# Attention over 64 heads in a fused four-layer kernel: probabilities kept in PSUM, cut to 16-bit halves there and turned by one DMA a head in place of TensorE

## The reference, cut to what matters

```python
# B = 2, T = 512, hidden 512, 32 heads, 8 KV heads (G = 4 heads each), head size 128, causal, RoPE
q = rope(x @ Wq.T); k = rope(x @ Wk.T); v = x @ Wv.T
scores = einsum('bkgtd,bksd->bkgts', q, k) / sqrt(128)
attn = softmax(where(causal, scores, -inf))
out = einsum('bkgts,bksd->bkgtd', attn, v)
return out @ Wo.T
```

## Time and profile before

| | |
|---|---|
| median of the runs | 2485.62 us (2484.69 to 2487.72) |
| profiled execution, its own time | 2484.75 us |
| its span, first to last instruction | 2482.8 us |
| busy over the span | PE 96%, PEld 55%, DVE 72%, ACT 64%, POOL 50% |
| attention stage, from the first turn to the last ohi | 1624.1 to 2325.9 us |
| granted TensorE clock, mean | 0.986 |

### The profile page before, as it was taken

How to read it: one execution, slowest core, us unless ns; L and a number is a source line. 1 busy time by engine, 2 the same in 40 slices (tenths; PEclk the granted TensorE clock), 3 DMA queues, 4 the chain that set the end, 5 groups by cost and what they waited for, 6 DMA issues and landing times. The chain is left out here.

```text
span 2482.8 us, 48888 instructions
## 1 busy us (share of the span) xinstructions
PE 2378.8 (96%) x15424; PEld 1368.9 (55%) x15624; DVE 1787.9 (72%) x3234; ACT 1591.7 (64%) x3327; POOL 1232.0 (50%) x986
## 2 busy tenths in 40 slices
PE   6999999999999999999999998879999999999797
PEld 3555555555555555555555555445555555555443
DVE  6777777777777777777777776577777777788522
ACT  7676776776776776776776775265665656656422
POOL 4455555555555556556556459344434343454223
PEclk8999999999999999999999999999999999999999
DMA  7343343343343343343343341230110110100000
GB/s 248 108 129 111 108 128 111 108 133 105 113 132 107 110 133 109 106 137 109 102 140 109 119 151 56 103 124 1 43 43 1 44 44 1 43 18 1 1 0 34
DMA packets 113827, 218.79 MB, mean 88 GB/s; under 512 B 9632, under 2 KB 43040, under 8 KB 111360
## 3 DMA queue, kind: packets, MB, share of 16 engines
q1 hardware_dynamic: 113536, 215.28, 26.6%
HBM read 212.10 MB, written 3.15 MB: 87 GB/s over the span
## 5 line engine op out<-in xcount | busy, mean ns | idle before, releaser
L256 DVE SCALAR_TENSOR_TENSOR xc<-bank,taps,xc 128x511 f32<-128x511 f32 (+2 forms) x384 | 284.7, 742 | 44.6 <-ACT xc L243 27.4
L984 ACT ACTIVATE E<-wq,cst 128x128 f32<-128x128 f32 x1024 | 311.8, 390 | 2.2 <-PEq L298 2.2
L1268 POOL TENSOR_TENSOR xw<-xt,wdec 128x384 f32<-128x384 f32 x128 | 106.4, 832 | 327.3 <-DVE xt L1119 163.7
L1277 POOL TENSOR_TENSOR acc<-acc,sq 128x512 f32<-128x512 f32 x112 | 172.0, 1536 | 186.8 <-ACT sq L996 186.8
L1911 POOL TENSOR_TENSOR qT<-qT,qrot 128x512 f32<-128x512 f32 x64 | 81.3, 1270 | 368.6 <-DVE qrot L1801 368.6
L1161 DVE SCALAR_TENSOR_TENSOR u<-xc,D,bank 128x512 f32<-128x512 f32 x128 | 95.6, 747 | 210.3 <-PE bank L813 198.8
L1100 DVE TENSOR_TENSOR E<-E,cbm 128x1024 f32<-128x1024 f32 x128 | 242.9, 1898 | 0.8
L61 PE MATMUL bank<-xhi,wx 128*128 128x512 f16 x640 | 242.5, 379 | 0.0
L60 PE MATMUL bank<-xlo,wx 128*128 128x512 f16 x640 | 242.5, 379 | 0.0
L59 PE MATMUL bank<-xhi,wx 128*128 128x512 f16 x640 | 242.5, 379 | 0.0
L1263 POOL TENSOR_TENSOR ecs<-ecs,xcC 128x768 f32<-128x768 f32 x128 | 234.1, 1829 | 0.4 <-POOLq L298 0.4
(11 more groups left out here) (237 smaller groups left out, 6299.4 us busy)
## 6 DMA issues: line engine op xcount, KB each, us to landing
wq<-cs_rows SPq DMA_DIRECT2D x128, 512.0 KB, 4.1
ecs<-ecs_rows SPq DMA_DIRECT2D x128, 384.0 KB, 3.6
wx<-in_w_xbc SPq DMA_DIRECT2D x80, 256.0 KB, 2.7
wz<-in_w_z SPq DMA_DIRECT2D x64, 256.0 KB, 2.7
wo<-in_w_o SPq DMA_DIRECT2D x64, 256.0 KB, 4.0
wq<-in_wq SPq DMA_DIRECT2D x8, 1024.0 KB, 5.7
awo<-in_wo SPq DMA_DIRECT2D x8, 1024.0 KB, 5.0
wkv<-in_wkv SPq DMA_DIRECT2D x8, 512.0 KB, 3.7
```

Source lines behind the costliest of these rows:

```text
L256: self.nc.vector.scalar_tensor_tensor(out=dst[:, d:T], in0=self.k.bank[bank][:, 0:T - d], scalar=self.taps[:, bass.ds(g, 1), b, j, 3 - d:4 ...
L984: ins = nc.scalar.activation(E[t.i % 4][:, h, c], sc.csr[t.i % 2][:, h, c * P:(c + 1) * P], ACT.Relu, scale=-1.0, bias=head(sc.cst, t, c, h))
L1277: nc.gpsimd.tensor_tensor(acc[t.b][:], acc[t.b][:], sq[:], ALU.add).then_inc(acc_done, 1)
```

## The change

1. Exponentials are written over the scores in PSUM (`scores_at`), and there are two homes for scores, one for even and one for odd heads (`S_AT`), in banks 2 to 6. The float32 probs in SBUF and `normalise` are gone.
2. ScalarE makes the leading halves straight from PSUM with the reciprocal as scale (`leading_p`), four instructions; VectorE makes the remainders, `rest_of_p`, four `scalar_tensor_tensor`: row block 1 at once, since the next scores share its bank, and the others after `maxima`.
3. Both halves go into one tile ph of 20 blocks of 128 columns, and one `dma_start_transpose` a head, issued by SP (`turn`), turns it into pt. TensorE's `turn`, pthi and ptlo are gone. `attend` reads pt; the remainders of one key block are five blocks apart.
4. New orders. TensorE: projection of Q, scores of n + 2, projections of K and V, output projection, attend. ScalarE: leading halves of p of n + 1, of q of n + 3, exps of n + 2, (k and v), and then ohi of n. VectorE: scales of n + 1, remainder of row block 1, rotation of q, maxima of n + 2, remaining remainders of n + 1, (k and v), addition of the output, and olo of n last.
5. The leading half of v comes straight from PSUM on ScalarE, its remainder from PSUM on VectorE in place of a copy; GpSimd's `rest_of_v` is gone.
6. SP's loads of SwiGLU weights are cut up, one or so an item in the first two groups, between transposes; the scale of the down projection is loaded in the SwiGLU stage, and VectorE multiplies it there later.

```diff
-P_OFF = [896, 1024, 512, 0]
-S_AT = [(3, 384), (4, 0), (3, 0), (2, 0)]
-T_OFF = [0, 512, 896, 1152]
-T_AT = [(5, 0), (6, 0), (5, 0), (5, 256)]
+P_BLOCKS = 20
+S_AT = [[(3, 384), (4, 0), (3, 0), (2, 0)], [(6, 384), (4, 256), (6, 0), (5, 0)]]
+HALVED = (1, 3, 2, 0)
...
-        pthi, ptlo = sb("pthi", [P, 1280], F16), sb("ptlo", [P, 1280], F16)
+        ph = [sb(f"phalves{i}", [P, P_BLOCKS * P], F16) for i in range(2)]
+        pt = [sb(f"pturned{i}", [P, P_BLOCKS, P], F16) for i in range(2)]
...
+        def leading_blocks(h, i):
+            return ph[h % 2][:].rearrange("p (b t) -> p b t", t=P)[:, i + 1:6 * i + 2:5, :]
+        def scores_at(h, i):
+            bank, at = S_AT[h % 2][i]
+            return k.bank[bank][:, at:at + (i + 1) * P]
+        def probs(h, i):
+            return scores_at(h, i).rearrange("p (b t) -> p b t", t=P)
...
+                def turn(n, h):
+                    sp.wait_ge(p_lo, n + 1)
+                    sp.sem_inc(step, 1)
+                    if not (isinstance(n, int) and n < 2):
+                        sp.wait_ge(pv_ready, n - 1)
+                        sp.sem_inc(step, 1)
+                    sp.dma_start_transpose(out=pt[h % 2][:], in_=ph[h % 2][:]).then_inc(pt_in[h % 2], 16)
...
                 def body(g, s, p):
+                    for b in range(NB):
+                        for h in range(QH):
+                            n = item(g, b, h)
+                            if later(g, b, h, 1):
+                                turn(n + 1, h + 1)
+                            if isinstance(g, int) and g < 2:
+                                load_swiglu(k, io, sp, n)
...
-                def scores(n, g, b, h, first=False):
+                def scores(n, g, b, h):
                     pe.wait_ge(q_lo, n + 1)
...
-                    if not first:
-                        pe.wait_ge(exp_done, n)
+                    wait(pe, p_lo, n - 1)
                     for i in (3, 2, 0, 1):
+                        if i == 1:
+                            wait(pe, p_lo1, n)
...
-                def attend(n, g, b):
+                def attend(n, g, b, h):
                     pe.wait_ge(pv_free, n + 1)
+                    pe.wait_ge(v_lo, (g * NB + b) + 1)
+                    pe.wait_ge(pt_in[h % 2], 16 * turned(g, b, h) + 16)
                     for j in range(CH):
...
+                        out = k.bank[7][:, j * P:T].rearrange("p (i t) -> p i t", t=P)
+                        mm = product(nc, out, (vhi[b][:, j], vlo[b][:, j]),
+                                     (pt[h % 2][:, 6 * j + 1:5 * j + 5], pt[h % 2][:, 6 * j:16 + j:5]), j == 0, j == CH - 1)
...
                             n = item(g, b, h)
-                            turn(n, h, [0], None)
-                            turn(n, h, [1], None)
-                            uses = ring_uses(g, b, h)
-                            for i, (kind, what) in enumerate(uses):
+                            for i, (kind, what) in enumerate(ring_uses(g, b, h)):
                                 ahead, bank = ring(g, b, h, i)
+                                ring_free(pe, ahead)
                                 if kind == "o":
...
                                     output(1 - b, bank, s if b else 1 - s, what)
+                                else:
...
+                                if kind == "q":
+                                    m = later(g, b, h, 2)
+                                    scores(item(*m), *m)
...
+                            attend(n, g, b, h)
...
-                def normalise(n, h):
+                def leading_p(n, h, of_parity):
                     act.wait_ge(exp_done, n + 1)
                     act.wait_ge(rsum_done, n + 1)
...
+                    wait(act, pt_in[h % 2], 16 * of_parity)
+                    for i in HALVED:
+                        nc.scalar.activation(leading_blocks(h, i), probs(h, i), ACT.Copy,
+                                             scale=rsum[h % 2][:, i:i + 1]).then_inc(p_hi, 1)
...
-                            for u, (bank, at, size) in enumerate(EVAC):
-                                if u == 2 and later(g, b, h, 1):
-                                    normalise(n + 1, h + 1)
-                                act.wait_ge(pt_ready, 3 * n + u + 1)
-                                nc.scalar.copy(pthi[:, at:at + size], k.bank[bank][:, 0:size]).then_inc(pt_hi, 1)
+                            if later(g, b, h, 1):
+                                leading_p(n + 1, h + 1, turned(g, b, h + 1))
                             if later(g, b, h, 3):
                                 leading_q(n + 3, h + 3)
+                            if later(g, b, h, 2):
+                                exps(n + 2, h + 2)
                             if h == 1 and not is_last(g, b):
                                 leading_k(g * NB + b + 1, 1 - b)
-                                leading_v(g * NB + b + 1, 1 - b)
+                                leading_v(g * NB + b + 1, 1 - b, *ring(g, b, h, 2))
                             act.wait_ge(pv_ready, n + 1)
                             nc.scalar.activation(ohi[b][:, h], k.bank[7][:, :], ACT.Copy,
                                                  scale=1.0 / P_SCALE).then_inc(ohi_done, 1)
-                            if later(g, b, h, 2):
-                                exps(n + 2, h + 2)
...
+                def rest_of_p(n, h, first):
+                    for i in HALVED[:1] if first else HALVED[1:]:
+                        dve.wait_ge(p_hi, 4 * n + (4, 1, 4, 2)[i])
+                        out = ph[h % 2][:, 5 * i * P:(6 * i + 1) * P].rearrange("p (b t) -> p b t", t=P)
+                        ins = nc.vector.scalar_tensor_tensor(out=out, in0=probs(h, i), scalar=rsum[h % 2][:, i:i + 1],
+                                                             in1=leading_blocks(h, i), op0=ALU.mult, op1=ALU.subtract)
+                    ins.then_inc(p_lo1 if first else p_lo, 1)
...
                                 scales(n + 1, h + 1)
-                            for u in range(2):
-                                rest_of_p(n, u)
+                                rest_of_p(n + 1, h + 1, True)
...
                                     serve(kind, ahead, bank, n + 3, 0, what[1], what[2])
...
                                 maxima(n + 2, h + 2)
+                            if later(g, b, h, 1):
+                                rest_of_p(n + 1, h + 1, False)
+                            for i, (kind, what) in enumerate(uses):
+                                ahead, bank = ring(g, b, h, i)
+                                if kind in "kv":
+                                    serve(kind, ahead, bank, 0, g * NB + b + 1, what[1], 0)
+                                elif kind == "o":
+                                    add_output(1 - b, ahead, bank, what, g * NB + b - 1)
                             dve.wait_ge(ohi_done, n + 1)
```

More of the change, by code:

```diff
@@ L1572, in ring, with ring_free @@
                 ahead -= QH
-            return (g * NB + b) * 10 + (PRO + ahead), (PRO + ahead) % 2
+            return (g * NB + b) * 10 + (PRO + ahead), k.bank[(PRO + ahead) % 2]
+        def ring_free(pe, ahead):
+            wait(pe, proj_free, ahead - 1)
         LAST_OUT = (NG * NB - 1) * 10 + (PRO - QH) + 5
@@ L1691, in body @@
-                            turn(n, h, [2, 3], 3 * n + 1)
-                            m = later(g, b, h, 2)
-                            if m:
-                                scores(item(*m), *m)
-                            attend(n, g, b)
-                            for i, (kind, what) in enumerate(uses):
-                                if kind == "o":
-                                    ahead, bank = ring(g, b, h, i)
-                                    pe.wait_ge(proj_free, ahead - 1)
@@ L1887, in body @@
                                                            op1=ALU.subtract).then_inc(pv_free, 1)
-                            for i, (kind, what) in enumerate(uses):
-                                if kind == "o":
-                                    ahead, bank = ring(g, b, h, i)
-                                    add_output(1 - b, ahead, bank, what, g * NB + b - 1)
                             if is_last(g, b):
@@ L2226, in program @@
                 attention(k, io, aw)
-            swiglu(k, out)
+            swiglu(k, io, out)
 def layouts(i):
```

194 lines of the change are left out of this document (83 added, 111 removed).

## The result

The changed kernel takes 2531.97 us (median of 4 runs, 2531.91 to 2532.07) against 2485.34 before (median of 4, one more than in the table above), a ratio of 1.0186 with a 95% interval of 1.0168 to 1.0204. It is slower by 46.6 us, where 2475 us, faster, was forecast; the range of 2440 to 2550 holds it. Spans differ by 2530.1 - 2482.8 = 47.3 us. The last ohi shows that all of it arises in the attention stage: it starts 49.2 us later than in the earlier trace rows.

A forecast was written before the change was run, and what follows sets the result against it. TensorE, busy 9.69 of 9.75 us, was taken as the bound, then a 9.5 us loop through the other engines. The attention stage's -10.3 us took 2484.75 to 2474.4; with 0.87 for the median, 2475 us, range 2440 to 2550.

The forecast's parts named there:

- What goes on TensorE: Ten turns (1.10 us) and a stall (0.1 us) leave each head: ordinary head 8.57 us on TensorE, some 77 us in all.
- the rival in which it keeps the pace: TensorE still bounds the attention stage: gain up to 77 us, 2408 us, or in part 2440; chance 0.12.
- The new loop: Chain through ScalarE, VectorE and GpSimd, exps through ohi to nmx, closes once a head: 9.5 us an ordinary head, against 9.75.
- The head with K and V: Output projection waits for the bank of k, then takes 2.72 us: head 15.55 us, against 14.96 before.
- The DMA transpose: 640 KB a head on SP's queue lands in 6 us (bounds 3.0 and 13.6), hidden up to 8.4 us.
- a late landing: Transpose lands later than 8.4 us and delays attend: 2507 us at a 10 us landing, 2568 at 13.6; chance 0.22.
- a bound queue: Transposes on SP's queue become the bound, 12.3 us a head, 787 us in place of 707: 2565 us; chance 0.06.
- Both ends: Attention stage from start to end: nmx(7) at 1685.5, last ohi at 2315.6 instead of 2325.9, that is -10.3 us.
- the interval before the last head: From nmx(62) to nmx(63), with moments (0.9 us) and no rotation (2.34 us): from 2292.7 to 2300.7.
- the loop longer than read: ScalarE and VectorE in the same banks as TensorE cost 0.3 us a head or more: 2490 to 2510 us; chance 0.13.

The follow-up runs named there:

- experiment 7: Changed kernel with attend right behind the scores, ohi ahead of exps, olo ahead of the output's addition: 2493.65 us; further variants added ring-order, GpSimd and last-unit changes.
- Experiment 2: Changed kernel with GpSimd's weight split ahead of the addition of q, and its remainder of q waiting until nmx is done: 2512.40 us.
- experiment 3: Changed kernel with the projection of V computed twice, filling TensorE's wait for the bank of k: 2513.71 us.
- experiment 4: Changed kernel with the ring in the order q, output, k, v instead of q, k, v, output: 2500.45 us.
- experiment 6: Changed kernel with each head's DMA transpose made twice, one after the other, attend waiting for the second: 2590.72 us.

## Why the prediction was wrong, by its own steps

- **What goes on TensorE** was right: 88% busy, not the bound. The rival in which it keeps the pace (2408 to 2440) did not come.
- **The new loop** was right as a mechanism (experiment 7), wrong in size: 10.1 us against 9.5. By terms, from the rows of after: exps to ohi 2.03 (2.02 forecast), so the exponentials in PSUM cost what those into SBUF did; ohi 0.63, olo 0.61, sums and reciprocal 0.38, to ScalarE and back 0.17 and 0.50 (0.09 and 0.45), row block 1 0.40, rotation 2.27 (2.34), and mask to nmx 2.58 + 0.51 where the sum had 2.61 with nmx in it. The term that failed is the last: nmx was priced from one row, which starts (1854.59) just as GpSimd's split ends there (1854.65), so the row doesn't show what nmx costs a little earlier in the split. That it can be longer was there to be read before the change: 20 of the 64 took 0.4 to 1.65 us. Experiment 2 gives 0.33 us of the 0.6 back (10.11 to 9.78). The rest is small latencies: 0.13 between the mask and the reductions, 0.08 and 0.05 above.
- **The head with K and V** was right in its structure, the output projection behind the bank of k, and in size in three heads of fourteen (15.8 against 15.55). In the other eleven it failed where that projection was priced at 2.72 us: behind 2.7 us of idle time the clock was at its lower level and it took 3.9 to 4.3. That is +1.6 of the +1.93 us, and experiments 3 and 4 confirm it from both sides: with the idle time filled, or without it, the clock is 1.00.
- **The DMA transpose** was right: 4.9 us measured, 6 taken, within 3.0 and 13.6, hidden. The rivals of a late landing and of a bound queue did not come. The Trainium skill (VectorE: DVE Perf Modes, The three transpose paths) has 1309 ns for a block, by which twenty would be an estimated 26 us; the trace doesn't agree, 4.9 us for twenty blocks. By the Trainium skill's other rule (Advanced Engine Details and Errata, X-Bar Transpose (TRN2)), 350 to 400 GB/s, they would move in an estimated 1.6 to 1.9 us, which is nearer: 640 KB in 4.9 - 1.3 = 3.6 us, with the fixed part of the earlier trace rows, is some 180 GB/s.
- **Both ends.** nmx(7) ends at 1689.8 (1685.5 forecast), 4.3 late; 13 units at 47.6 instead of 44.05 add 46.4; the last unit's heads 3.5; the interval before the last head 12.8 instead of 8.06, 4.7; the rest 0.6. Together 59.5, from 2315.6 to 2375.1. Of the 46.4, the clock is 10 x 1.6 = 16, the long nmx 12.6 (summed over these units), the second pass of the loop 4.6, for which the sum had nothing, and the rest, some 13, the small latencies of every head; the 4.3 and this rest weren't tried apart. The failed step in the interval is a queue that the moved step was not followed past: GpSimd's layer norm stands behind the moments, qlo(63) behind that, and the last scores behind qlo. The prediction had named the moments as VectorE's work only, and its 8.06 is below even the 11.2 us of the kernel before, where this wait already stands in the trace; 3.1 of the 4.7 us are that, and 1.6 came with olo's new place.
- **The rivals.** The one nearest to the result is the loop longer than read (chance 0.13, 2490 to 2510), but it counted the ordinary heads alone, and its reason, three engines in the same banks, is not what experiment 2 found. Of the 3.7 us that a unit with a long K/V head takes beyond the forecast, 1.8 are the three ordinary heads and 1.9 the K/V head; neither alone would have given 2532.

The common cause is that prices came from rows in which nothing was in the way: nmx behind GpSimd's instruction instead of beside it, matmuls without idle time ahead of them, and a last interval without its wait.

## What to carry to other kernels

When a change lifts the load from the engine that sets the pace, compute the new loop through the other engines before the gain; here 77 us of TensorE time bought nothing, since the loop through VectorE and ScalarE stood just below. Price a small VectorE instruction on that loop from the shortest and the longest of its group, with the GpSimd instruction that may run beside it, and a stretch of matmuls behind a wait of some 2.6 us at either clock; here eleven of fourteen had the lower one. When two gains don't add, or add to too much, count the heads of each kind in every trace before looking for a new cause. Order the ring so that what is ready goes first, and follow each moved instruction through every queue that waits for it, the special bodies of the last unit too.

## What the runs showed of the hardware

- A VectorE `tensor_scalar` of four columns from SBUF to SBUF that is issued while a GpSimd instruction runs ends when that one ends: 0.51, 0.55, 1.48 us instead of 0.17, three pairs of ends within 0.04 us, and so for all 47 that were met in the changed kernel. The four reductions, which read PSUM, took 1.69 us beside the split in the changed kernel and the same in experiment 2 without it. The Trainium skill (SBUF — State Buffer, Who interferes with whom) says that GpSimd shares one pair of VectorE's SBUF ports, that `tensor_scalar` is among the operations that can take this pair, and that the later one waits for the whole of the other. The trace agrees, with the numbers above.
- After 2.60 to 2.68 us of idle time TensorE's granted clock fell in eleven K/V heads of the changed kernel, to 0.62 over the 4.5 us from 1882.40, its matmuls 0.43 us apart; after 2.28, 2.60 and 2.65 us it stayed at 1.00 in three. In experiment 2, after 2.6 to 2.7 us, it fell in eight heads and held in five, and after 1.8 it held. In experiment 6, after 4.7 us, the head had 0.79.
- A transpose of 640 KB from SBUF to SBUF keeps SP's queue for 3.1 us and lands 4.9 us after its issue. Two in a row take 11.1.
- Exponentials written over the scores in PSUM took 2.03 us a head in all, those into SBUF 2.02, though the record of the 512-column one is shorter (0.66 us against 0.69 in the earlier trace rows).
- Where a loop of the program starts its second pass VectorE stood idle 4.47 us in the changed kernel and 3.14 in the kernel before, with no wait that the profile shows.
